# Cross-attention and ternary feed-forward kernel on one core: weight preparation earlier, token scales on GpSimd, a second halving of the softmax sums

## What is computed

```python
def _rmsnorm(x, g):
    return g * (x * jax.lax.rsqrt(jnp.mean(x * x, axis=-1, keepdims=True) + EPS))

def _act_quant(x):
    scale = 127.0 / jnp.clip(jnp.max(jnp.abs(x), axis=-1, keepdims=True), 0.0001, None)
    y = jnp.clip(jnp.round(x * scale), -128, 127) / scale
    return y

def _ternary_quant(w):
    s = jnp.mean(jnp.abs(w))
    return jnp.round(jnp.tanh(w / (s + EPS))) * jnp.arctanh(s)

def _linear_bit(x, w, g):
    return jnp.einsum('bsd,od->bso', _act_quant(_rmsnorm(x, g)), _ternary_quant(w))

x = x + cross_attention(layernorm(x), ctx, Wq, Wkv_expand, Wout)   # 16 heads of 16, causal mask, 64 keys
h = silu(_linear_bit(layernorm(x), w1, g1)) * _linear_bit(layernorm(x), w2, g2)   # 256 -> 1024
x = x + _linear_bit(h, w3, g3)                                     # 1024 -> 256
```

## Time and profile before

| | us |
|---|---|
| median of 3 runs (lowest, highest) | 218.42 (217.4, 219.26) |
| the profiled execution's own time | 218.21 |
| its span in the trace | 216.5 |
| outside the span | 1.7 |
| DVE busy, ACT busy, POOL busy, PE busy | 179.7, 140.9, 129.2, 156.2 |
| mean granted clock of TensorE, as a share of full speed | 0.897 |

### The profile page before, as it was taken

One profiled execution on the slowest core, in us unless ns is written; L12 is line 12 of the kernel. 1 busy time (PEld: TensorE's weight loads), 2 busy tenths in 40 slices (PEclk: granted clock), 3 DMA queues, 4 the chain that ended last, 5 costly groups with the idle time before them and its releaser, 6 DMA issues.

```text
span 216.5 us, 3808 instructions
## 1 busy us (share of the span) xinstructions
PE 156.2 (72%) x1194; PEld 106.3 (49%) x1194; DVE 179.7 (83%) x339; ACT 140.9 (65%) x192; POOL 129.2 (60%) x197
## 2 busy tenths in 40 slices
PE   6996775883964978765698694486488887786463
PEld 6574544652753757553586361133265544443341
DVE  1279594978899799999996989999969999999950
ACT  2123669423684558978978979297679878687421
POOL 4061526138564265672544478799797999999510
PEclk9999699998895799999589998569969999999955
DMA  5999900000000000000000000000000001000011
GB/s 157 313 424 407 362 13 3 0 2 0 0 6 0 0 0 0 3 0 0 2 3 0 0 0 0 3 0 24 26 27 26 26 24 48 24 24 33 26 41 48
DMA packets 6159, 11.33 MB, mean 52 GB/s; under 512 B 512, under 2 KB 4864, under 8 KB 5632
## 3 DMA queue, kind: packets, MB, share of 16 engines
q1 hardware_dynamic: 5920, 10.75, 14.0%
q10 hardware_dynamic: 224, 0.39, 0.7%
HBM read 9.04 MB, written 2.10 MB: 51 GB/s over the span
## 4 chain that ended last, share of the span: by engine, by line
DVE 38%; PE 18%; issue 17%; ACT 14%; POOL 7%; DMA 3%; DVEq 1%; ACTq 0%; POOLq 0%
DVE hh L1099 5%; DVE c_max L1117 5%; DVE row_max L865 4%; PE bank L523 4%; DVE m_x L970 4%; POOL u L372 3%; ACT probs L702 3%; DMA wkvT<-in_wkvT 3%; DVE u_max L962 3%; PE bank L452 3%; PE bank L640 3%; DVE probs L871 3%; ACT q_x L735 3%; DVE row_sum L878 2%; PE bank L561 2%
## 5 line engine op out<-in xcount | busy, mean ns | idle before, releaser
L354 POOL TENSOR_TENSOR half_sum<-probs 128x512 f32<-128x512 f32 x16 | 20.7, 1295 | 42.0 <-ACT probs L702 37.2
L391 POOL TENSOR_TENSOR c_h<-hh,g3b 128x1024 f32<-128x1024 f32 x15 | 35.3, 2356 | 5.3 <-DVE hh L1099 4.4
L621 PE MATMUL wide<-wT,xqT 128*128 128x512 bf16 x128 | 33.4, 405 | 5.9 <-DVE hh L1099 5.6
L640 PE MATMUL bank<-wT,hT 128*128 128x256 bf16 x128 | 19.1, 299 | 12.8 <-ACT hT L801 12.8
L796 ACT ACTIVATE sq_junk<-hh,root_x 128x1024 bf16<-128x1024 f32 x16 | 18.3, 1146 | 14.8 <-DVE hh L1099 14.8
L702 ACT ACTIVATE probs<-probs,ln_rstd 128x1024 f32<-128x1024 f32 x16 | 18.3, 1150 | 12.2 <-DVE probs L871 12.2
L523 PE MATMUL bank<-woutT,attnT 128*128 128x256 f32 x64 | 19.2, 452 | 9.4 <-DVE attnT L886 9.4
L372 POOL TENSOR_TENSOR u<-xc,g 128x512 f32<-128x512 f32 x16 | 20.1, 1280 | 5.6 <-ACT q_x L735 5.6
L640 PEld LDWEIGHTS bank<-wT,hT 128*128 128x128 bf16 x128 | 12.1, 105 | 22.2 <-ACT hT L801 17.5
L621 PEld LDWEIGHTS wide<-wT,xqT 128*128 128x128 bf16 (+1 forms) x128 | 12.3, 102 | 20.1 <-issue 7.2
L801 ACT ACTIVATE hT<-bank,round_c 128x1024 bf16<-128x1024 int16 x16 | 17.6, 1098 | 5.5 <-PE bank L561 5.5
(11 more groups left out here) (119 smaller groups left out, 332.0 us busy)
## 6 DMA issues: line engine op xcount, KB each, us to landing
out<-y SPq DMA_DIRECT2D x16, 128.0 KB, 1.7
xT<-in_xT SPq DMA_DIRECT2D x1, 1280.0 KB, 16.9
x_sb<-in_x SPq DMA_DIRECT2D x1, 1280.0 KB, 21.0
w_in<-in_w1T SPq DMA_DIRECT2D x1, 1024.0 KB, 10.4
w_in<-in_w2T SPq DMA_DIRECT2D x1, 1024.0 KB, 12.2
w_in<-in_w3T SPq DMA_DIRECT2D x1, 1024.0 KB, 14.2
xT<-in_xT SPq DMA_DIRECT2D x1, 512.0 KB, 7.5
x_sb<-in_x SPq DMA_DIRECT2D x1, 512.0 KB, 8.4
```

The lines of the kernel that those rows point to most:

```text
L391: g.tensor_tensor(out=c_h[:, t, :], in0=hh[:, t, :], in1=g3b[:], op=ALU.mult).then_inc(c_ready, 1)
L621: last = nc.tensor.matmul(wide[:, (w * 2 + n) * 512:(w * 2 + n + 1) * 512], xqT_cols(T, w * DC + c), w_cols[:, c, n * 512:(n + 1) * 512], ...
L640: last = nc.tensor.matmul(down_banks[t][:, 0:D], hT[:, t, n, :], w_cols[:, n, :], start=(n == 0), stop=(n == HC - 1))
```

## The change

It has five parts.

1. Weight work earlier. SP loads the three matrices earlier (w1 ahead of the second xT, x of batches 1 and 2 last). ACT takes the sums of absolute values of w1 and w2 ahead of the first exponentials and that of w3 right behind them. PE's matmul for the sums goes to bank4 in iteration 0. DVE computes the scales before `sums(0)`, `arctanh_terms` and `ternary(0)` right after `shift(1, 1)` and before batches 3 and 4 are measured, `ternary(1)` after iteration 1 and before batches 5 to 7 are measured, `ternary(2)` and `log_branch` after iteration 2. ACT's tanh stands after its iterations 0, 1 and 2, `Ln` after the second tanh.
2. Token scales. The scale min(127 / max, 127 * factor / CLIP) takes the place of 127 * factor / max(max * factor, CLIP). DVE only takes the reciprocal of the maximum (`token_recip`); POOL makes a bound (`fb_bound`) in `factor`, and the scale itself in `token_scale`, first thing in its iteration, and in the slots of tiles 1 and 3 last thing. DVE's `dequant` makes the scales that silu and square need: for batches 0 to 4 in one piece in the transition, behind `sums(7)` and `residual(6)`; for 5, 6 and 7 one at a time.
3. A second halving on POOL, in place, over both tiles at once (`quarter_ready`), so that DVE reduces 16 numbers for each head.
4. DVE's `sums(j)` stands between the two maxima of iteration j, and behind `divide(j - 1)`; it stood ahead of both.
5. Small orders: first query ahead of the first values, scores(0) ahead of the second, batches 1 and 2 measured after the values are copied; 6 warming matmuls in place of 8; loops over iterations 3 and 4 written out on DVE and POOL.

The core of the diff:

```diff
@@ SP @@
+                load_w(0, w1T_d)
                 load_xT(1, 2).then_inc(xT12_in, 16)
+                load_w(1, w2T_d)
+                load_w(2, w3T_d)
                 load_x(1, 2).then_inc(x12_in, 16)
@@ POOL @@
-                    last.then_inc(half_ready, 1)
+                    need(pool, half_ready, 2 * b + 2)
+                    g.tensor_tensor(out=half_sum[:, :, :, 0:SK // 4], in0=half_sum[:, :, :, 0:SK // 4],
+                                    in1=half_sum[:, :, :, SK // 4:SK // 2], op=ALU.add).then_inc(quarter_ready, 1)
...
+                    g.tensor_tensor(out=fb_bound[:], in0=fb_a[:, bass.ds(b * TB, TB)], in1=over_clip[:],
+                                    op=ALU.mult).then_inc(fbb_ready, 1)
+
+                def token_scale(b):
+
+                    need(pool, rmx_ready, b + 1)
+                    need(pool, fbb_ready, b + 1)
+                    need(pool, qx_ready, 2 * b)
+                    for t in range(TB):
+                        last = g.tensor_scalar(qs_x[:, t, :], rm_x[:, t, :], 127.0, fb_bound[:, t:t + 1], ALU.mult, ALU.min)
+                    last.then_inc(qsx_ready, 1)
...
                 def iteration(j):
+                    if from_(j, 3):
+                        token_scale(j - 3)
@@ ACT @@
+                act.wait_ge(const_set, 3)
+                weight_sums(0)
                 query_copy(1)
-                act.wait_ge(rstd_done, 2)
+                weight_sums(1)
+                act.wait_ge(rstd_done, 1)
                 exponentials(0, 0)
                 exponentials(0, 1)
+                weight_sums(2)
+                act.wait_ge(rstd_done, 2)
...
+                act.wait_ge(inv_ready, 1)
+                weight_tanh(0)
                 act.wait_ge(rstd_done, 3)
                 iteration(1)
+                weight_tanh(1)
+                act.wait_ge(ln_in, 1)
+                a.activation(w_ln[:], w_ln[:], ACT.Ln).then_inc(ln_out, 1)
                 act.wait_ge(rstd_done, 4)
                 iteration(2)
-                act.wait_ge(inv_ready, 1)
-                weight_tanh(0)
+                weight_tanh(2)
                 with act.Fori(3, 5) as j:
                     iteration(j)
-                weight_tanh(1)
                 iteration(5)
-                weight_tanh(2)
@@ DVE @@
+                def token_recip(b):
                     need(dve, u_max_ready, b + 1)
...
+                    need(dve, qsx_ready, b)
+                    v.reciprocal(rm_x[:].rearrange("p t w -> p (t w)"),
+                                 u_max[:, bass.ds(b * 2 * TB, 2 * TB)]).then_inc(rmx_ready, 1)
+
+                def dequant(b, n):
+
+                    dve.wait_ge(u_max_ready, b + n)
+                    dve.wait_ge(b_a, b + n)
+                    tiles, cols = slice(b * TB, (b + n) * TB), slice(b * 2 * TB, (b + n) * 2 * TB)
+                    v.tensor_tensor(m_x[:, tiles, :], u_max[:, cols].rearrange("p (t w) -> p t w", w=2),
+                                    fb_a[:, tiles].unsqueeze(2).to_broadcast([P, n * TB, 2]), ALU.mult).then_inc(mx_ready, n)
...
+                    v.scalar_tensor_tensor(out=dq_x[:, cols].rearrange("p (t w) -> p t w", w=2), in0=m_x[:, tiles, :],
+                                           scalar=CLIP, in1=w_ath[:, 0:2].unsqueeze(1).to_broadcast([P, n * TB, 2]),
+                                           op0=ALU.max, op1=ALU.mult).then_inc(dqx_ready, n)
```

More of the change, by code:

```diff
@@ L429, in slot @@
                     scales(T, t, b)
+                    if t == 1 and late(b + AHEAD):
+                        token_scale(b + AHEAD)
                 half_sums(0)
@@ L437, in _ @@
                 iteration(2)
-                with pool.Fori(3, 5) as j:
+                for j in range(3, B - 1):
                     iteration(j)
-                iteration(5)
-                iteration(6)
+                token_scale(4)
                 values(7)
@@ L444, in _ @@
                 scaled(5)
+                token_scale(5)
                 pool.wait_ge(w_down_ready, 1)
@@ L756, in iteration @@
                     probs_T_copy(j, 1)
-                    if isinstance(j, int) and j == B - 3:
-                        act.wait_ge(ln_in, 1)
-                        a.activation(w_ln[:], w_ln[:], ACT.Ln).then_inc(ln_out, 1)
                     if live(j + 1):
@@ L928, in _ @@
                 values_copy(6, 4)
-                v.memset(w_tmp[:], 0.0).then_inc(bank4_free, 1)
+                v.memset(w_tmp[:], 0.0)
+                dve.wait_ge(x12_in, 16)
+                for b in (1, 2):
+                    measure(b)
+                    aggregate(b)
                 steps = [0]
@@ L968, in scales_1 @@
+                def token_recip(b):
                     need(dve, u_max_ready, b + 1)
-                    for t in range(TB):
-                        last = v.tensor_scalar(m_x[:, t, :], u_max[:, t, :], fb_a[:, t:t + 1], CLIP, ALU.mult, ALU.max)
-                    last.then_inc(mx_ready, 1)
-                def scales_3(b):
-                    need(dve, mx_ready, b + 1)
-                    v.reciprocal(rm_x[:], m_x[:]).then_inc(rmx_ready, 1)
-                    if late(b):
-                        product_scales(b, 1, m_x[:])
-                    else:
-                        v.tensor_copy(m_ahead[:, bass.ds(b * 2 * TB, 2 * TB)],
-                                      m_x[:].rearrange("p t w -> p (t w)")).then_inc(m_kept, 1)
@@ L983, in scales_4 @@
-                def scales_4(b):
-                    need(dve, rmx_ready, b + 1)
-                    need(dve, qx_ready, 2 * b)
-                    for t in range(TB):
-                        last = v.tensor_scalar(qs_x[:, t, :], rm_x[:, t, :], 127.0, fb_a[:, t:t + 1], ALU.mult, ALU.mult)
-                    last.then_inc(qsx_ready, 1)
-                    if late(b):
-                        root_scales(b, 1)
-                def product_scales(b, n, m):
-                    v.tensor_tensor(dq_x[:, b * 2 * TB:(b + n) * 2 * TB].rearrange("p (t w) -> p t w", w=2), m,
-                                    w_ath[:, 0:2].unsqueeze(1).to_broadcast([P, n * TB, 2]),
-                                    ALU.mult).then_inc(dqx_ready, n)
@@ L1014, in iteration @@
                     front = from_(j, 2)
-                    sums(j)
                     if from_(j, 1):
@@ L1018, in iteration @@
                     maximum(j + 1, 0)
+                    sums(j)
                     maximum(j + 1, 1)
@@ L1030, in iteration @@
                         token_max(j - 2)
-                        scales_1(j - 2)
-                    if from_(j, 1) and not front:
+                    elif from_(j, 1):
                         need(dve, b_bn, 2)
@@ L1072, in arctanh_terms @@
                                            op1=ALU.mult).then_inc(ln_in, 1)
-                iteration(0)
+                dve.wait_ge(wsum_done, 1)
+                step(v.tensor_scalar(w_s[:], bank4[:, 0:3], 1.0 / (H * D), None, ALU.mult))
+                step(v.tensor_scalar(w_inv[:], w_s[:], 1e-8, None, ALU.add))
+                v.reciprocal(w_inv[:], w_inv[:]).then_inc(inv_ready, 1)
+                sums(0)
+                maximum(1, 0)
+                maximum(1, 1)
+                shift(1, 0)
+                shift(1, 1)
+                arctanh_terms()
+                ternary(0)
                 dve.wait_ge(x_in, 16)
@@ L1079, in _ @@
                 iteration(1)
-                weight_scales()
+                ternary(1)
                 for b in range(5, B):
@@ L1084, in _ @@
                 iteration(2)
-                arctanh_terms()
-                with dve.Fori(3, 5) as j:
+                ternary(2)
+                log_branch()
+                for j in range(3, B - 1):
                     iteration(j)
-                ternary(0)
-                iteration(5)
-                ternary(1)
-                log_branch()
-                kept_product_scales(0, 4)
-                iteration(6)
                 def gated(T, t):
```

132 lines of the change are left out of this document (57 added, 75 removed).

## The result

The changed kernel takes 225.04 us (median of 6 runs, 223.52 to 228.93); the kernel before 218.70 in the same comparison (6 runs, 217.40 to 219.27). The ratio is 1.0297, 95% interval 1.0247 to 1.0346: 3.0% slower, where 221.5 us, 1.4%, had been forecast. The side was right, and the time is inside the range of 214.5 to 226, but the size is twice what was said.

A forecast was written before the change was run, and what follows sets the result against it. The prediction took DVE's own work (busy 179.7 of 216.5 us) as the main bound. Milestones reached +3.8 us, the rest -0.7: +3.1 on 218.21 gives 221.3, plus 0.2 for the median 221.5 us; range 214.5 to 226.

The forecast's parts named there:

- Milestone 1: Start to end of shift(1, 1): ACT's added sums and POOL's second halving delay the first row sum, +1.8 us.
- Milestone 2: Up to divide(0): a chain of weight work, measuring, row scales and recipT now leads to it; step +3.7, running total +5.5 us.
- milestone 3: divide(0) to divide(1): 16.65 us where before took 14.42, DVE idling twice; step +2.2, running total +7.7 us.
- 3.1 us more for stalls: Ahead of divide(0): arctanh_terms, 2.4 us itself, stalled by POOL's half sums and second halving; bounds 2.1 and 3.6 us.
- Milestone 4: divide(1) to divide(2): 13.5 us where before took 16.18, which had arctanh_terms in it; step -2.6, running total +5.1 us.
- Milestone 5: divide(2) to end of exp(7, 1): shorter rounds without tanh, Ln loads and log branch save 5.5 us; running total -0.4 us.
- the loop named in the prediction: Rounds before exp(7, 1): exponential, half sum, second halving, token scales, q_x, copies and exponentials; 11.25 us, with hops 11.5.
- Milestone 6: exp(7, 1) to gated(1): ACT waits for dequant behind the last row sum; 18.5 us for 14.3, running total +3.8 us.
- The rest: After gated(1): slots of tiles 1 and 3 gain 0.35 us each, nothing changes from tile 4 on; -0.7 us.
- The relief of DVE wins: First rival, 17%: new waits of milestones 1 to 4 and 6 fall into slack, giving 212.2 us.
- The stalls behind POOL don't come: Second rival, 20%: DVE's small steps slip between POOL's instructions, giving +0.7 us, 219.1 us.
- TensorE cools down: Third rival, 13%: DVE's waits in iterations 0 to 2 idle PE and slow project steps, +3 to +5, 225.5 us.

The follow-up runs named there:

- e1: Changed kernel with POOL's row scales of batches 1 and 2 behind half_sums(0) instead of keys(0): 224.95 us, ratio 1.0328.
- e5: Changed kernel with 8 warming matmuls instead of 6, nothing else: 223.23 us, ratio 1.0232.
- e8: Kernel before with 6 warming matmuls instead of 8, nothing else: 218.97 us, ratio 1.0018.
- e3: Changed kernel with batches 3 and 4 measured ahead of arctanh_terms and ternary(0), 5 to 7 ahead of ternary(1): 220.24 us, ratio 1.004.
- e4: Changed kernel without POOL's second halving, so DVE reduces 32 numbers of each head again: 220.42 us, ratio 1.012.
- e2: Changed kernel with dequant of batches 0 to 3 ahead of DVE's iteration 6, batch 4 left in the transition: 221.65 us.
- e7: Changed kernel with the four edits of e1, e2, e3 and e5, and without the second halving: 210.10 us, ratio 0.9638.
- e12: The same kernel as e7, unchanged, run again in another group: 211.58 us, ratio 0.9682.
- e6: Changed kernel with the four edits of e1, e2, e3 and e5 together, second halving kept: 213.08 us, ratio 0.9785.
- e10: Kernel before with the second halving on POOL alone added: 221.82 us.

## Why the prediction was too small

**The step that failed** is "Milestone 1, the end of shift(1, 1): +1.8 us". It was +7.2 in the profiled execution and +3.9 with a warm start. It followed ACT's added sums and the second halving only, and missed two edits of part 5, both of which it priced at nothing without saying so. (a) The measuring of batches 1 and 2 was moved behind the value copies, and POOL's queue carries its waiter ahead of the keys: 2.6 us, by e1. Part 5 names this move, on DVE; what had to be asked was who is queued behind `row_scales` on POOL. Without it the warm step is +1.2, close to the +1.8 said. (b) Six warming matmuls in place of eight: part of the executions begin with TensorE at its lower clock. At this milestone the profiled one is 3.4 us behind e5, and e8's is 6.1 us behind before. The medians point the same way, 225.0 for e5's 223.2, but the intervals of the two ratios overlap, so what (b) costs in the median is not well known.

**Milestone 2 (+3.7 said, +3.5 in e5) and milestone 3 (+2.2, +3.1)** were right in mechanism: divide idles for `recipT`, and `recipT` for `ln_rstd`, behind batches measured too late:

```profile
46.91 0.59 ACT L725 COPY recipT<-bank 128x512 f32<-128x512 f32 x1 [5.03 <-POOL ln_rstd L323]
64.35 0.59 ACT L725 COPY recipT<-bank 128x512 f32<-128x512 f32 x1 [4.40 <-POOL ln_rstd L323]
```

e3 takes the time of both back, though DVE's second wait stays. Milestone 2's "3.1 us more for stalls" is 2.6 in the changed kernel: `arctanh_terms` takes 5.0 us (37.34 to 42.34) where 2.4 were reckoned without stalls. In milestone 3, `xc` took 1.64 us where e3 has 0.62.

**Milestone 4 (-2.6, -1.9)** was right in size.

**Milestone 5 (-5.5 said, -3.5 measured)** was too hopeful. The last three rounds were said to take 11.5, 11.5 and 13.2 us, and took 13.3, 11.4 and 13.0. The one that differs holds the project step of 3.40 us, at a granted clock of 0.57, where before had 1.95 at full clock; it appears with the second halving and goes without it (e4). The exponential behind divide(2) ended 0.4 us later than said. Whether the loop named in the prediction sets the round is not shown: without the halving of 1.28 us in it the steady round is 11.2 us for 11.4. In the warm kernel this miss, 2.0 us, is as large as that of milestone 1, 2.1 us.

**Milestone 6 (+4.2, +5.0)** was right: ACT idle for 5.15 us ahead of the table load, released by `dq_x`, as said (4.65 reckoned), and e2 gives 4.2 us of the transition back. The 0.8 us above the forecast were inside its bounds.

**The rest (-0.7 said, -5.1 measured)** was wrong, and hid 4.4 us of the other misses; that the time still lay inside the range is luck to that extent. 1.1 us are the slots of tiles 1 and 3 (6.77 for 7.62, 7.44 for 7.71), where -0.7 was said. 1.6 us are one slot (4.30 for 5.94) and 1.9 the final stretch (14.1 for 16.0). The final stretch of before and of after; a row has the stretch, its length, the busy time of PE, weight loads, DVE, ACT and POOL, then the granted clock and the DMA's share and rate:

```profile
200.52:216.50 15.98, 7.53 (x53) 5.09 (x50) 8.51 (x15) 4.47 (x5) 3.36 (x12) 0.67 0.10 34
```

```profile
210.38:224.50 14.12, 6.20 (x53) 4.55 (x50) 8.51 (x15) 4.48 (x5) 3.34 (x12) 0.85 0.12 39
```

Same instruction counts, same time on DVE, ACT and POOL; only PE is slower, at a granted clock of 0.67 for 0.85 (in the slot 0.71 for 1.00). So 3.5 us of the -5.1 are clock and not work of another order. Where they come from is open. The profiles of one kernel, e7 and e12, differ in both stretches (5.94 and 4.94 us, 14.1 and 16.1), so an execution can change them. But the changed kernel and e1 to e5, six profiles, all have the short forms, and the run times speak against mere chance: of the 50 runs of the kernel before none is more than 1.7 us under the profiled one, though 3.5 us were to be had, and the six runs of e5 are 0.8 us apart.

The signs named for "right" are all in the changed profile: the two waits above, 0.91 us of idle DVE ahead of the second `wT`, divide(2) at 79.36, 11.4 us from exp(5, 1) to exp(6, 1), the wait ahead of the table load, and the longer `xc`. None of them looked at the start, where the largest miss lay.

**The rivals.** "The relief of DVE wins" did not come true in this kernel, but e6 shows that the change beats the kernel before once three orders and the start of TensorE are mended. Its halving does not carry that (e4, e7, e10); which of the other parts does was not run apart. "The stalls behind POOL don't come" is refuted, by `xc` at 14.8 us for 5.3. Here the Trainium skill (SBUF — State Buffer, "Who interferes with whom") had the mechanism: GpSimd and certain VectorE operations lock each other out for a whole instruction. The trace agrees, with every lengthened `xc` ending just behind a POOL instruction. Of 4.3 us saved on row sums, e10 shows 3.4 back in `xc`, which the prediction had named as the heir but had not priced. "TensorE cools down" came true in part, and its 225.5 us are nearest to the measured time: project(0), behind 5 us of idle PE, takes 3.78 us where before took 1.99, and project(3) 3.40; project(1) was as slow already. But it had looked for the cost in iterations 0 to 2, not at the start and in the round of project(3).
